# Products of probabilities and values in blocks of eight instead of four

## What is computed

```
scores = q @ k.T * scale      # 512 x 512, causal or key mask
att    = softmax(scores)
y      = att @ v              # 512 x 16
```

## Time and profile before

| | |
|---|---|
| median of three runs | 1317.51 us |
| the profiled execution | 1315.83 us, span 1314.1 us |
| PE busy | 1137.6 us (87%) |
| DVE busy | 1011.7 us (77%) |
| ACT busy | 685.4 us (52%) |
| POOL busy | 511.2 us (39%) |
| granted clock, mean | 0.936 |

### The profile page before, as it was taken

How to read it: one execution, slowest core, us unless ns; L and a number is a source line. 1 busy time by engine, 2 the same in 40 slices (tenths; PEclk the granted TensorE clock), 3 DMA queues, 4 the chain that set the end, 5 groups by cost and what they waited for, 6 DMA issues and landing times. The chain is left out here.

```text
span 1314.1 us, 22048 instructions
## 1 busy us (share of the span) xinstructions
PE 1137.6 (87%) x7592; PEld 677.8 (52%) x7592; DVE 1011.7 (77%) x2733; ACT 685.4 (52%) x1363; POOL 511.2 (39%) x712
## 2 busy tenths in 40 slices
PE   5589999999999999999999999999984116999994
PEld 2454555545555554444545454544333005988984
DVE  6588888888887889898989898988833884676651
ACT  6035555554545656666666666666760103566551
POOL 5556475574755443223232332411021013444432
PEclk9669999999998999999999999999997556999997
DMA  5551542534416435152524333243012303644422
GB/s 170 112 114 31 117 105 58 114 80 100 114 50 146 118 94 114 50 113 65 114 86 109 91 87 98 73 93 79 2 49 85 113 5 100 172 105 111 109 25 24
DMA packets 90480, 118.06 MB, mean 90 GB/s; under 512 B 13089, under 2 KB 60257, under 8 KB 90242
## 3 DMA queue, kind: packets, MB, share of 16 engines
q1 hardware_dynamic: 84226, 108.12, 32.2%
q0 software_dynamic: 6144, 8.52, 3.9%
HBM read 48.76 MB, written 16.91 MB: 50 GB/s over the span
## 5 line engine op out<-in xcount | busy, mean ns | idle before, releaser
L748 ACT ACTIVATE probs<-ps_st 128x512 f32<-128x512 f32 (+3 forms) x1024 | 476.3, 518 | 339.7 <-PE ps_st L589 335.7
L609 PE MATMUL ps_p<-kst,qst 63*128 63x512 f32 (+3 forms) x1024 | 384.1, 434 | 16.7 <-DVE mx L836 11.6
L589 PE MATMUL ps_st<-qst,kst 64*128 64x512 f32 (+3 forms) x1024 | 359.1, 418 | 8.6 <-ACT probs L748 7.5
L834 DVE TENSOR_REDUCE mx<-ps_p 128x1 f32<-128x512 f32 x512 | 322.3, 680 | 13.2 <-PE ps_p L609 11.8
L589 PEld LDWEIGHTS ps_st<-qst,kst 64*128 64x128 f32 x1024 | 164.8, 186 | 259.5 <-ACT probs L748 201.1
L570 PE MATMUL ps_o<-probs,vals 128*32 128x512 f32 (+3 forms) x2048 | 232.9, 527 | 13.8 <-POOL probs L480 13.8
L836 DVE CUSTOM_DVE_ANT_0 ps_p<-ps_p,tri 128x128 f32<-128x128 f32 (+3 forms) x512 | 237.6, 514 | 8.2 <-PE ps_p L609 7.1
L609 PEld LDWEIGHTS ps_p<-kst,qst 63*128 63x128 f32 x1024 | 171.5, 188 | 45.4 <-DVE mx L836 19.7
L427 POOL TENSOR_SCALAR lnw<-mv 128x4 f32<-128x4 f32 x24 | 4.8, 198 | 347.5 <-DVE mv L820 347.5
L480 POOL TENSOR_SCALAR_AFFINE_SELECT probs<-probs 128x512 f32<-128x512 f32 x128 | 79.2, 634 | 87.9 <-ACT probs L748 87.5
L1199 PE MATMUL moe_ps_y<-moe_w,moe_hid_h 128*128 128x256 f32 x512 | 94.6, 283 | 0.0
(11 more groups left out here) (204 smaller groups left out, 1872.0 us busy)
## 6 DMA issues: line engine op xcount, KB each, us to landing
qst<-qk_h SPq DMA_DIRECT2D x64, 256.0 KB, 4.7
kst<-qk_h SPq DMA_DIRECT2D x64, 256.0 KB, 5.0
qst<-qk_l SPq DMA_DIRECT2D x32, 256.0 KB, 5.5
kst<-qk_l SPq DMA_DIRECT2D x32, 256.0 KB, 5.1
moe_w1r<-in_w_dram SPq DMA_DIRECT2D x8, 1024.0 KB, 5.6
moe_w2r<-in_w_dram SPq DMA_DIRECT2D x8, 1024.0 KB, 8.9
xin<-in_x_dram SPq DMA_DIRECT2D x8, 512.0 KB, 4.5
xres<-in_x_dram SPq DMA_DIRECT2D x8, 512.0 KB, 3.9
```

The source lines that it names most:

```text
L589: last = nc.tensor.matmul(out, kst[rows, t % 2, pair, kt * P:(kt + 1) * P], qst[rows, t % 2, pair, lo:S], start=True, stop=not masked)
L609: last = nc.tensor.matmul(ps_p1[:, i % 3, 0:keys], qst[rows, t % 2, pair, qt * P:(qt + 1) * P], kst[rows, t % 2, pair, 0:keys], start=True ...
L748: nc.scalar.activation(probs[:, kt, j, 0:n], ps_st[:, i % 2, 0:n], ACT.Exp, scale=float(DH) ** -0.5).then_inc(exp_done, 1)
L834: nc.vector.tensor_reduce(mx[:, g % 2, at:at + 1], bank, AX.X, ALU.max).then_inc(max_done, 1)
```

## The change

The key of the value steps in the written-out order is changed. Before, the blocks of the key tiles 0, 1, 2, 3 of a group stood at units -2, 2, 6, 10 of the next group. After, tiles 0 and 1 both stand at -2 and tiles 2 and 3 both at 6. The blocks of kt = 1 and kt = 3 thus come four units earlier on every engine that has a part in them, and the copy of `ps_o` by ScalarE, which stands at the last of them, comes four units earlier too.

```diff
     for g in range(NG):
         for kt in range(TT):
             for j in range(GH):
-                put(16 * (g + 1) + 4 * kt - 2, "pv", g, kt, j)
+                put(16 * (g + 1) + 8 * (kt // 2) - 2, "pv", g, kt, j)
```

## The result

The changed kernel takes 1376.97 us (median of 4 runs, 1370.57 to 1385.69) against 1317.83 us of the kernel before, a ratio of 1.0456 with a 95% interval of 1.039 to 1.0523: 59 us slower. The forecast was 1353, slower, with a range up to 1376. The sign was right, the number was too low by 24, and the measured time lies just above the range.

What follows compares the result with a forecast made beforehand. PE's order of work sets the pace, DVE close behind, ACT the slower engine in runs of units. Cross groups 19 us plus self groups 18 make 37 on the profiled 1315.8: 1353 us, range 1328 to 1376.

Steps and rivals of the forecast that it cites:

- part 1: Value blocks on PE: a double block lasts 1.86 us, each merge saves 0.14 us, 128 merges 18 us.
- part 2: Units 0 to 3 of each group: ACT's exponentials make four units take 2.09 us instead of 1.32, +0.77 per group.
- part 3: Units 6 to 11 around one M step: 3.3 us, or 3.8 with an input copy; +0.7 cross, +0.1 self.
- part 4: Right behind a double block: PE's waits for DVE vanish, the largest being 0.68 us above a plain pair.
- parts 5 and 6: Group sums: cross +0.6 us (+0.3 to +0.9), times 32 is 19 us; self +0.55, times 32 is 18 us.
- the walk through one group: One cross group, first block to M step: 8.20 us becomes 9.19, +0.99, or +0.75 after 0.25 comes back.
- part 7: Other waits: triangles have 0.3 us spare, and more PE idling costs no clock, from the tail at 1.00.
- DVE takes over: Rival: double blocks leave DVE idle, 9.8 us per cross turn, making the turn 68.5 us, total 1384 us; chance 0.12.
- What the changed profile would show: Signs: value rows 1.92 us, runs about 2.1, cross turn 65, self 55.2, PE's ACT wait +30 us, ACT busy unchanged.
- Faster: Rival: PE's order alone decides and ACT keeps up in runs of four; 128 merges give 1298 us; chance 0.06.
- it cancels: Rival: both double blocks give back 0.6 us each and the self loop has slack; 1316 to 1321 us; chance 0.05.

## Why the forecast was right and where it was wrong

**Joined blocks (part 1).** Right: 1.85 to 1.86 us for sixteen records of 512 columns in every group, 0.14 us less than two.

**Four units in a row (part 2).** Right in its number: 2.10 us in most groups, up to 2.29, against 2.09. That ACT is the last to hold it is right too, but it is not alone: with half the exponentials 1.94 remains, with both halved 1.67, and of the 3.3 us of a cross turn only 1.2 went when ACT was fast. The cause was read too narrowly, and the number held because ACT is the slowest of three limits that lie close together. "Nothing on PE can shorten this" was right for the order as it stands; the half projection in the middle could.

**Units 6 to 11 (part 3).** 3.37 and 4.08 us where 3.3 and 3.8 were said. The 0.1 in the self half is too low for the stretch itself: it takes 2.72 us in three of the four groups, where it took 2.73 to 2.90 with a block of 0.36 in it, so +0.2 to +0.35. With only tiles 2 and 3 joined three of the four groups kept their length all the same.

**What comes back (part 4).** Right where it was: pairs behind a double block take 0.66 to 0.68.

**The sums (parts 5 and 6).** A cross turn +3.3 where 4 x 0.6 = 2.4 was said, a self turn +1.4 where 4 x 0.55 = 2.2 was said. The four cross groups grew by 0.5, 1.1, 1.3 and 0.5 us: two of them lie above the +0.9 that was taken as the most, and in one of these the pair at units 4 and 5, which the walk through one group took as plain, takes 1.02 us. The rotary groups came out at +0.63 (13.28 against 12.65 us) for +0.62; the two other self groups changed by -0.1 and +0.2 where +0.3 to +0.7 was said, since their waits behind a block gave back nearly all. The two errors cancelled, and that the waits came to 38 us against 37 is luck.

**The clock (part 7).** This is the step that failed: "a few per cent more idling on PE costs no clock". It rested on one row, the tail at 1.00 with 21.7 of 25 us busy. In the changed kernel the tail turns had 0.92 and 0.91, and turns 7, 9, 11 and 12 lost some too: 60 us at the lower level against 19, some 18 us of time in the profiled execution and more in the slower runs; the kernel with a quarter of its value work left out lost 3.5 us in one self turn alone. A single stretch in which the clock had held was no bound on what it costs when it doesn't. With 18 us the number would have been 1371, and the measured execution was 1372.8. So the term that was put at nothing is the miss; why the clock falls where it does stays open.

**DVE takes over.** This rival gave 1384, near the measured 1377, but not by its mechanism: in the steady cross turn DVE's idle time ahead of maxima is 3.3 us (1.2 before), not 9.8, and the turn at full clock is 65.6, not 68.5. It is the second limit in a run, as the halved exponentials showed, and where a cut projection took ACT's wait away PE waited 0.48 us for DVE instead.

**What the changed profile would show.** The value rows of 1.92 us, the wait in each run and the run of 2.1 us are there. PE's wait for ACT grew by 43 us where 30 was said, ACT's busy time by 8 where it was to stay; the cross turn is 65.6 for 65, the self turn 54.4 for 55.2.

**Faster; it cancels.** Both out. Even with exponentials and maxima halved the joined order stays 31 us behind.

## What to carry over

When PE feeds two engines through two or three banks each, its other work is what spaces the products; the busy shares (ACT 64%) say nothing of that. Before two blocks of such work are joined, ask what now stands next to each other in the place that one of them leaves, and take the cost from the chain score, hand-over, exponential: here 0.77 us lost for 0.14 won. And where a change adds waits on PE, leave room for its clock above the sum, priced from rows where it fell, not from a row where it held: here 0.34 to 0.5 us for each us at the lower level, while how much time it spends there could not be told from the waits.

## What was not expected of the hardware

Work taken off PE made the kernel slower: 57 us less of products, +14 us of time, by 50 us more at 1.2 GHz. The granted clock fell in turns 9, 11 and 12 of the changed kernel and held in turns 10 and 13, with the same share of PE busy by the profile in all five, 93 to 94%: the share does not tell them apart. And the position of single drops moved when copies of products filled the waits in front of them, while their number hardly changed.
